# Moving scores between the steps of attention, and assigning PSUM banks by release times, in a cross-attention and FFN kernel

## The reference

```python
x = x + xattn(layernorm(x), ctx, ctx)      # scores / sqrt(32), softmax over 512 keys, times values
x = x + ffn(layernorm(x))                  # gated low-rank experts: the best of 8 by a gate
```

## Time and profile before

| | us |
|---|---|
| median of 3 runs | 1023.92 (1020.99 to 1025.22) |
| the profiled execution, its own time | 1022.49 |
| its span in the trace | 1020.7 |
| TensorE busy | 947.1 (93%) |
| VectorE busy | 902.3 (88%) |
| GpSimd busy | 801.6 (79%) |
| ScalarE busy | 730.8 (72%) |

### The profile page before, as it was taken

The page is one execution under the profiler, slowest core; times in us unless marked ns, Lnnn a source line. Parts: engine busy times, 40 slices in busy tenths (PEclk is TensorE's granted clock), DMA queues, the critical chain, the costliest instruction groups (busy, mean ns, idle before and its releaser), DMA issues.

```text
span 1020.7 us, 24586 instructions
## 1 busy us (share of the span) xinstructions
PE 947.1 (93%) x9518; PEld 371.1 (36%) x9518; DVE 902.3 (88%) x1106; ACT 730.8 (72%) x1301; POOL 801.6 (79%) x454
## 2 busy tenths in 40 slices
PE   4789999999999999999999999999999999999996
PEld 3223333333333333333333323333222225777773
DVE  6979999999999999999999999998888886888976
ACT  5367788888888888888888877888777777554440
POOL 6259999999999999999999999999999998222110
PEclk9999999999999999999999999999999999999998
DMA  8674776767676767676867685756655744766423
GB/s 246 191 172 109 165 169 155 166 152 169 149 169 154 173 145 176 142 171 148 184 142 179 132 192 129 182 121 153 121 119 138 163 93 147 246 209 233 159 104 164
DMA packets 319875, 164.18 MB, mean 161 GB/s; under 512 B 182216, under 2 KB 307240, under 8 KB 319760
## 3 DMA queue, kind: packets, MB, share of 16 engines
q1 hardware_dynamic: 319456, 161.76, 64.3%
q0 software_dynamic: 304, 0.85, 0.4%
HBM read 107.58 MB, written 54.53 MB: 159 GB/s over the span
## 4 chain that ended last, share of the span: by engine, by line
PE 35%; DVE 31%; issue 25%; ACT 5%; POOL 3%; DMA 1%; SPq 0%; DVEq 0%; POOLq 0%; ACTq 0%
DVE row_max L927 14%; PE psum L590 8%; PE psum L604 6%; PE psum L617 5%; PE psum L735 5%; DVE den_t L939 4%; PE psum L552 4%; ACT probs L864 3%; PE psum L713 3%; DVE o_t L933 3%; DVE probs L1138 2%; PE psum L578 2%; DVE prod_mem L985 2%; PE psum L701 1%; ACT prod_mem L817 1%
## 5 line engine op out<-in xcount | busy, mean ns | idle before, releaser
L864 ACT ACTIVATE probs<-psum 128x512 f32<-128x512 f32 x1024 | 554.7, 596 | 131.0 <-PE psum L590 113.0
L927 DVE TENSOR_REDUCE row_max<-psum 128x4 f32<-128x2048 f32 x248 | 565.8, 2281 | 64.3 <-PE psum L552 64.0
L590 PE MATMUL psum<-q_stack,k_stack 97*32 97x512 f16 x4096 | 334.8, 386 | 9.9 <-issue 3.5
L365 POOL TENSOR_TENSOR sums<-probs 128x2048 f32<-128x2048 f32 x63 | 287.7, 4566 | 17.5 <-ACT probs L864 17.4
L353 POOL TENSOR_TENSOR sums<-probs 128x2048 f32<-128x2048 f32 x63 | 287.2, 4559 | 7.1 <-PE psum L627 5.5
L604 PE MATMUL psum<-probs,v_in 128*32 128x512 f32 x2048 | 268.8, 598 | 1.0
L590 PEld LDWEIGHTS psum<-q_stack,k_stack 97*32 97x32 f16 x4096 | 96.7, 95 | 258.8 <-ACT probs L864 149.2
L552 PE MATMUL psum<-high_mem 32*128 32x512 f16 x992 | 98.0, 384 | 23.7 <-DVE row_max L927 20.1
L325 POOL TENSOR_TENSOR o_t<-o_t,inv 128x512 f32<-128x512 f32 x64 | 67.2, 1049 | 40.7 <-DVE inv L945 38.8
L330 POOL TENSOR_TENSOR o_all<-o_all,o_t 128x512 f32<-128x512 f32 x64 | 81.6, 1274 | 9.2
L604 PEld LDWEIGHTS psum<-probs,v_in 128*32 128x32 f32 x2048 | 59.2, 110 | 60.9 <-issue 16.2
(11 more groups left out here) (119 smaller groups left out, 759.2 us busy)
## 6 DMA issues: line engine op xcount, KB each, us to landing
q_stack<-q_split SPq DMA_DIRECT2D x192, 128.0 KB, 3.4
xa<-in_x_dram SPq DMA_DIRECT2D x32, 512.0 KB, 4.7
o_all<-in_x_dram SPq DMA_DIRECT2D x256, 64.0 KB, 2.4
x_attended<-o_all SPq DMA_DIRECT2D x64, 256.0 KB, 4.1
out_dram<-probs SPq DMA_DIRECT2D x32, 512.0 KB, 2.9
q_split<-prod_mem SPq DMA_DIRECT2D x15, 1024.0 KB, 5.3
xa<-x_attended SPq DMA_DIRECT2D x16, 512.0 KB, 4.5
probs<-x_attended SPq DMA_DIRECT2D x16, 512.0 KB, 4.7
```

The source lines that it names most:

```text
L365: pool.tensor_tensor(sums[:, 2 * u % SUMS], probs[:, u % 2, 0], probs[:, u % 2, 1], ALU.add).then_inc(front_done, 1)
L590: last = pe.matmul(st_ps[row:row + D, bank_of["score", u, n], :], k_stack[:, u % SLOTS, t * P + row:t * P + row + D], q_stack[:, u % SLOTS ...
L864: act.activation(probs[:, s, keys, g, :], st_ps[:, bank_of["score", u, n], :], ACT.Exp, scale=EXP_SCALE).then_inc(exped, 1)
L927: dve.reduce_max(row_max[:, u % 2, t:G * ST:ST], s_ps[:], AX.X).then_inc(reduced, 1)
```

## The change

Three things change in the tables that set the order and the banks; nothing that is computed does.

1. `BEGIN` and `MIDST`: the quarters of an even step had 4, 5, 4, 3 scores and have 4, 5, 3, 4. Those of an odd step had 4, 4, 4, 4 and have 5, 5, 3, 3. `NORM_AT` stays at 13.
2. The bank of a fill is chosen by a time in quarters at which each earlier use is held to be read (0.4 of a quarter for scores and maxima, 0.95 for a part of x, a given quarter for denominators), where before it was a count of fills.
3. The second and third part of an x tile no longer have to take the bank of the first.

```diff
--- before.py
+++ after.py
@@ -193,35 +193,39 @@
             tile_of = lambda u: (u + AHEAD) // 2 + FIRST
             whole = lambda n: FIRST <= n < TILES
 
-            BEGIN = ((0, 4, 9, 13, NSC), (0, 4, 8, 12, NSC))
-            MIDST = ((2, 6, 11, 15), (2, 6, 10, 14))
+            BEGIN = ((0, 4, 9, 12, NSC), (0, 5, 10, 13, NSC))
+            MIDST = ((2, 6, 11, 14), (2, 7, 12, 15))
             NORM_AT = 13
             DOWN_AT, FOLD_AT = ((-AHEAD, ST - 1), (1 - AHEAD, 0)), (1 - AHEAD, ST - 1)
 
-            filled = [("part", n, i) for n in range(FIRST) for i in range(PIECES)]
+            QUARTERS_KEPT = {"score": 0.4, "max": 0.4, "part": 0.95}
+            DEN_TAKEN_AT = (ST + 0.95, 3.95)
+            filled = [(-LEAD, ("part", n, i)) for n in range(FIRST) for i in range(PIECES)]
             for u in range(-AHEAD, UNITS + 2):
                 for t in range(ST):
                     scores = [("score", u, n) for n in range(BEGIN[u % 2][t], BEGIN[u % 2][t + 1])] if live(u) else []
                     half = MIDST[u % 2][t] - BEGIN[u % 2][t]
+                    now = []
                     if u % 2 == 1 and t < PIECES and whole(tile_of(u)):
-                        filled.append(("part", tile_of(u), t))
-                    filled += scores[:half]
+                        now.append(("part", tile_of(u), t))
+                    now += scores[:half]
                     if t == 2 and live(u + 1):
-                        filled.append(("max", u + 1, 0))
-                    filled += scores[half:]
+                        now.append(("max", u + 1, 0))
+                    now += scores[half:]
                     if t == (ST - 1 if u % 2 == 1 else 2) and live(u - 1):
-                        filled.append(("den", u - 1, 0))
-            KEPT = {"score": 2, "max": 2, "den": (5, 5), "part": 6}
-            bank_of, bank_before, free_at, last_in = {}, {}, [0] * BANKS, [None] * BANKS
-            for i, use in enumerate(filled):
+                        now.append(("den", u - 1, 0))
+                    filled += [(u * ST + t + (i + 1) / (len(now) + 1), use) for i, use in enumerate(now)]
+            bank_of, bank_before, free_at, last_in = {}, {}, [-LEAD] * BANKS, [None] * BANKS
+            for i, (at, use) in enumerate(filled):
                 bank = min(range(BANKS), key=lambda b: free_at[b])
-                if use[0] == "part" and use[1] >= FIRST and use[2] > 0:
-                    bank = bank_of["part", use[1], use[2] - 1]
                 bank_of[use] = bank
                 if last_in[bank] is not None:
                     bank_before[use] = last_in[bank]
-                kept = KEPT["den"][use[1] % 2] if use[0] == "den" else KEPT[use[0]]
-                free_at[bank], last_in[bank] = max(i, free_at[bank]) + kept + 1, use
+                if use[0] == "den":
+                    free_at[bank] = (use[1] + 1) * ST + DEN_TAKEN_AT[use[1] % 2]
+                else:
+                    free_at[bank] = max(at, free_at[bank]) + QUARTERS_KEPT[use[0]]
+                last_in[bank] = use
 
             spare = [i for i in range(BANKS) if i != bank_of["den", UNITS - 1, 0]]
             y_ps = s_ps.rearrange("p (t c) s -> p t (c s)", t=2).rearrange("p t (c m) -> p t c m", m=P)
```

## The result

The change makes the kernel slower: 1059.0 us median of 4 runs (1057.47 to 1061.41) against 1024.57 (4 runs, 1020.99 to 1025.65), ratio 1.0345 with a 95% interval of 1.0311 to 1.0378. The profiled execution took 1057.47 us, its span is 1055.7 us against 1020.7.

What follows compares the result with a forecast made beforehand. The prediction held the kernel bound by the time from one VectorE reduce to the next, in a ring with TensorE and ScalarE. +31.5 us over 26 pairs and -1.2 at the end, on 1022.49, gave 1053 us (1028 to 1066).

Steps and rivals of the forecast that it cites:

- What sets the pace: Across a pair's eight quarters: the time from one VectorE reduce to the next sets the pace, 25.32 us a pair before.
- Even 2: Third quarter of an even step: one score fewer, bound by TensorE, 3.08 us from reduce to reduce against 3.34.
- Even 3: Last even quarter: the normalisation, no longer hidden, delays exp 13, score 15 and the reduce; 4.23 us, 1.39 more.
- Odd 0 and odd 1: First two odd quarters: five scores each wait for exps two ahead; 3.41 and 3.59 us, 0.24 and 0.66 more.
- Odd 2 and odd 3: Last two odd quarters: one score fewer each, 2.97 and 2.90 us, 0.47 and 0.35 less.
- The bank table: In odd 0, x's first part now follows the denominators in its bank; this was to cost nothing.
- The last pairs: Last six pairs, without parts or normalisation: even 2 and odd 3 win, even 3 loses; -0.2 us each, -1.2 together.
- The sum: Whole kernel: 1.21 us more on 26 pairs, less 1.2 at the end, +30.3 on 1022.49, taken as 1053.
- the case in which ScalarE catches up in the odd step: Even 3 costs 1.39 us but odd 0 and odd 1 stay at 3.17 and 2.93: 1030 us, chance 0.10.
- no stall: Even 3 only 3.10 us, the odd step's costs as forecast: 1023.5 us, chance 0.05.
- The faster rival: Only the cuts in even 2, odd 2 and odd 3 count, 1.08 us a pair: 993 us, chance 0.07.
- GpSimd passed nothing on: Worse rival: GpSimd passes exp 15's delay to the next pair's denominators, 0.8 us a pair: 1074 us, chance 0.05.

Runs made afterwards that it cites:

- f1: The changed kernel with the normalisation of x's tile one place earlier, ahead of exp 12 (NORM_AT 12 for 13): 1030.99 us, 1.0076 of before.
- g4: The changed kernel with ScalarE normalising only the first 512 of 1024 columns of each x tile: 1047.32 us, 1.0249 of before.
- f2: The changed kernel with the even step's quarters put back to 4, 5, 4, 3: 1029.19 us, 1.0058 of before.
- g2: The changed kernel with even quarters 4, 6, 3, 3 and odd quarters 5, 4, 4, 3: 1009.75 us, 0.9879 of before.
- f4: The changed kernel with both steps' quarters as before, leaving the bank table and free banks for x's parts: 1023.08 us, 1.0000 of before.
- g1: The changed kernel with even quarters 4, 6, 3, 3 and odd quarters put back to 4, 4, 4, 4: 1014.56 us, 0.9925 of before.

## Why the prediction was right

The forecast was 1053 us (1028 to 1066), slower with a chance of 0.88; measured are 1059.0 us. Point by point:

- *What sets the pace.* Shown: the time goes where the reduces move apart, and the time of every kernel above follows from its quarters to within some 2.5 us. For the change the reduces show 25 whole pairs of 1.44 more, 36.0 us, and five behind them of 0.14 less, which take 0.7 off (the first of the 26 pairs with a normalisation lies ahead of them, in the start); the spans differ by 35.0. The first whole pair starts at 82.31 in the change and at 82.19 before.
- *Even 2*: forecast 3.08, measured 3.07.
- *Even 3*, the term that decides: forecast 4.23, measured 4.33. The mechanism is shown by f1 (moved, 1.21 less) and g4 (shorter by 0.43, 0.42 less). Of the 0.10 that is missing, 0.08 is the hand-over: I let an exp start 0.45 after its score, by one place in the trace of before; here exp 12 started 0.53 after it (380.70 to 381.23).
- *Odd 0 and odd 1*: forecast 3.41 and 3.59, measured 3.42 and 3.71. Shown by f2 to be their own. That the fifth score waits for the exp two ahead is read in the trace: 0.33 us before score 4 (386.91), 0.26 before score 9 (390.55), each straight ahead of L556. The size in odd 1 was short by 0.12. From L556 to L556 it is 3.64 (387.24 to 390.88) where I had counted 3.60; another 0.07 is that the reduce at 391.40 starts 0.52 after its L556 and not 0.45, and what makes that difference is open. Exp 4 comes late too, but it costs nothing: ScalarE is idle for 0.22 us between it and the high half of the part (388.26), and where exp 4 starts later still, 0.81 after its score (493.90 to 494.71), odd 1 is no longer.
- *Odd 2 and odd 3*: forecast 2.97 and 2.90, measured 2.91 and 2.97. Odd 2 is 2.98 from L556 to L556 (390.88 to 393.86), as counted; the 0.06 that are missing are those by which the reduce at its start came late. For odd 3 my own terms add up to 2.82, which I rounded up to the floor of VectorE; odd 3 is longer since its first score follows the last part of x and starts 0.48 after L556 (393.86 to 394.34) and not 0.33: VectorE frees that bank only then, with the low half that ends at 394.28. g2, where odd 2 is longer, has 2.81, the sum of the terms.
- *The bank table*: costed at nothing, and f4 shows nothing, 1.0000.
- *The last pairs*: -0.2 each was forecast, -0.14 measured; even 3 lost 0.36 there and not 0.26, and 0.08 of this is the same hand-over.
- *The sum*: a pair was forecast at 26.53 and is 26.75. The spans grew by 35.0 us, 4.7 more than the 30.3 of the forecast: 0.22 on 25 pairs is 5.5, the last pairs won 0.5 less than forecast, and against this I had counted 26 long pairs, where 25 count (1.2): an error that helped by luck. The rest of the way from 1053 to 1059 is that the profiled execution of the change, 1057.47, lies 1.5 us below the median.
- *Rivals*: the case in which ScalarE catches up in the odd step is excluded by f2; no stall and faster, by the trace itself. The faster rival named its own condition, another place for the normalisation or for score 12; f1 and g1 are that condition, and only g1 is faster, because f1 still pays for odd 0 and odd 1 and 3.12 in even 3. GpSimd passed nothing on: even 0 and even 1 keep 3.44 and 2.91 in every kernel.

## What to carry to other kernels

When work moves between quarters of a hand-written schedule, look at the other engines' queues for what stands at a fixed place beside it: here one instruction of 1.23 us was free as long as the score behind it came late, and cost 1.13 us of it once the score in front of it came late too. A queue's filler has to be moved with the gap that it fills. Count a quarter by the engine that ends it; taking a score from a quarter that ends in a wait for TensorE gave at least its 0.22 us on TensorE here (0.27 in even 2, 0.53 in odd 2), and giving it to one that VectorE ends is free while banks and exponentials keep up (six scores in even 1, not five in odd 1). In the bank table a score of even 1 in g1 waits for the exp three ahead, one of odd 1 for the exp two ahead; that this is the reason was not tried apart.

## What the runs showed of the hardware

How well the handshakes repeat was unexpected: a quarter that a change does not touch keeps its time within 0.01 to 0.02 us in all ten traces taken after that of before, but for single pairs. The start of an exp behind the score that it waits for is less even, 0.45 us at one place and 0.53 at others, and so is the start of a reduce behind its L556, mostly 0.45 and 0.52 in odd 2 of the change. What makes the difference is open and was not tried.
